# A selective scan with attention on one core: the order of exponential and u^T piece in ScalarE's queue

## The reference

```python
dt = softplus(proj[..., :512] + dt_bias)          # 512 channels
Bm, Cm = proj[..., 512:576], proj[..., 576:]       # 64 states
def step(hst, ins):
    dt_t, B_t, C_t, x_t = ins
    dA = exp(dt_t[:, :, None] * A)
    hst = hst * dA + (dt_t * x_t)[:, :, None] * B_t[:, None, :]
    y_t = einsum('bds,bs->bd', hst, C_t)
    return (hst, y_t)
```

## Time and profile before

| | us |
|---|---|
| median of 3 runs (3551.68 to 3552.13) | 3551.79 |
| the profiled execution, its time | 3553.52 |
| the profiled execution, its span | 3551.7 |
| of it busy: PE / VectorE / ScalarE / GpSimd | 3345.1 / 2983.3 / 2910.1 / 2304.6 |

### The profile page before, as it was taken

How to read it: one execution, slowest core, us unless ns; L and a number is a source line. 1 busy time by engine, 2 the same in 40 slices (tenths; PEclk the granted TensorE clock), 3 DMA queues, 4 the chain that set the end, 5 groups by cost and what they waited for, 6 DMA issues and landing times.

```text
span 3551.7 us, 59805 instructions
## 1 busy us (share of the span) xinstructions
PE 3345.1 (94%) x22946; PEld 2573.6 (72%) x22946; DVE 2983.3 (84%) x2916; ACT 2910.1 (82%) x4664; POOL 2304.6 (65%) x1066
## 2 busy tenths in 40 slices
PE   8998999899989999999999899999899989999999
PEld 5888888888888888988988888888787432222244
DVE  4988999899889989988999899899997488888241
ACT  5999999999998998999999999998896327777621
POOL 1878898898888879888988888798687000000000
PEclk9999999999999999999999999999899989999999
DMA  3222222222222222222222222222111052211000
GB/s 112 72 73 64 79 70 67 61 68 68 68 69 87 66 62 66 70 63 60 79 68 63 60 68 70 59 86 68 51 62 54 17 127 35 37 19 19 1 6 18
DMA packets 192638, 214.17 MB, mean 60 GB/s; under 512 B 75585, under 2 KB 144961, under 8 KB 192097
## 3 DMA queue, kind: packets, MB, share of 16 engines
q1 hardware_dynamic: 192354, 210.36, 20.6%
HBM read 192.19 MB, written 18.06 MB: 59 GB/s over the span
## 4 chain that ended last, share of the span: by engine, by line
PE 67%; ACT 19%; DVE 8%; issue 3%; POOL 2%; DMA 0%; SPq 0%; DVEq 0%; ACTq 0%; POOLq 0%
PE psum L1292 17%; PE psum L1513 16%; PE psum L1507 13%; PE psum L1504 10%; ACT arena L950 8%; ACT arena L933 6%; DVE arena L1198 4%; PE psum L1600 3%; PE psum L1589 3%; PE psum L1564 2%; DVE row_max L1245 2%; POOL arena L697 1%; PE psum L1533 1%; POOL arena L713 1%; ACT L950 1%
## 5 line engine op out<-in xcount | busy, mean ns | idle before, releaser
L1198 DVE TENSOR_TENSOR_SCAN arena<-arena,psum 128x512 f32<-128x512 f32 x2048 | 2379.0, 1229 | 192.1 <-ACT arena L950 105.8
L713 POOL TENSOR_TENSOR arena<-arena 128x1024 f32<-128x1024 f32 x1024 | 2237.5, 2192 | 458.1 <-DVE arena L1198 434.7
L950 ACT ACTIVATE arena<-arena,a_neg 128x512 f32<-128x512 f32 x2048 | 1436.5, 712 | 178.1 <-PE psum L1507 176.3
L1513 PE MATMUL psum<-ident,arena 128*128 128x128 f32 x8192 | 1244.4, 275 | 1.6 <-POOL arena L713 1.6
L933 ACT ACTIVATE arena<-arena,bT 128x512 f32<-128x512 f32 x1536 | 1091.9, 711 | 0.0
L1507 PE MATMUL psum<-ident,arena 128*128 128x128 f32 x6144 | 1021.7, 276 | 0.0
L1513 PEld LDWEIGHTS psum<-ident,arena 128*128 128x128 f32 x8192 | 974.8, 143 | 2.1 <-POOL arena L713 2.1
L1504 PE MATMUL psum<-arena 128*128 128x128 f32 x4096 | 844.5, 288 | 104.4 <-DVE arena L1198 89.8
L1504 PEld LDWEIGHTS psum<-arena 128*128 128x128 f32 x4096 | 656.2, 194 | 350.5 <-issue 185.6
L1507 PEld LDWEIGHTS psum<-ident,arena 128*128 128x128 f32 x6144 | 754.9, 144 | 0.0
L1292 PE MATMUL psum<-arena 128*128 128x512 f32 x1472 | 708.0, 604 | 29.4 <-ACT arena L813 18.3
(11 more groups left out here) (117 smaller groups left out, 1079.9 us busy)
## 6 DMA issues: line engine op xcount, KB each, us to landing
arena<-bc_dram SPq DMA_DIRECT2D x256, 512.0 KB, 3.7
arena<-diag_dram SPq DMA_DIRECT2D x224, 128.0 KB, 2.1
arena<-qk_dram SPq DMA_DIRECT2D x96, 128.0 KB
diag_dram<-arena SPq DMA_DIRECT2D x32, 256.0 KB, 4.5
qk_dram<-arena SPq DMA_DIRECT2D x12, 512.0 KB, 4.9
arena<-in_x SPq DMA_DIRECT2D x4, 512.0 KB, 10.9
arena<-in_up_w SPq DMA_DIRECT2D x1, 2048.0 KB, 11.7
out_xT<-arena SPq DMA_DIRECT2D x8, 256.0 KB, 2.2
```

What stands on the lines that cost most here:

```text
L713: pool.tensor_tensor(out[:, :, way], h_now[:, :, way], c_row, ALU.mult)\
L950: act.activation(decay[:, w % 2, f], dt_[:, u % 2, f], ACT.Exp, scale=a_neg[:, d, f, st:st + 1])\
L1198: dve.tensor_tensor_scan(hs[:, w % RING, f, rows][:, way], decay[:, w % 2, f, way], psum[:, 4 + n % U_BANKS, way], end_state(w - DS, f) if ...
L1513: return pe.matmul(psum[:, c, f * P:(f + 1) * P], hs[:, w % RING, f, at:at + P], ident[:, :], is_transpose=True, start=False, stop=w % DS ...
```

## The change

In each pair of ScalarE operations of the scan, `scan_input(w + 1, f)` is called ahead of the exponential of the same f instead of behind it:

```diff
                     if st == 0:
                         act.wait_ge(s["dt_ready"], NI + u)
                     for f in range(NI):
+                        if w + 1 < SCAN_TILES:
+                            scan_input(w + 1, f)
                         if w >= 2:
                             act.wait_ge(s["scan_done"], NI * (w - 2) + f + 1)
                         act.activation(decay[:, w % 2, f], dt_[:, u % 2, f], ACT.Exp, scale=a_neg[:, d, f, st:st + 1])\
                             .then_inc(s["decay_ready"], 1)
-                        if w + 1 < SCAN_TILES:
-                            scan_input(w + 1, f)
                     do(act_turns(u, st))
```

## The result

The changed kernel takes 3571.68 us (median of 5 runs, 3568.82 to 3576.25) against 3551.79 for the kernel before: a ratio of 1.0056, 95% interval 1.0042 to 1.0071. So it is slower by more than 0.2%, 5.3 us above the forecast and inside its range. The profiled execution has a span of 3569.9 us, 18.2 more than before.

The account below looks back on a forecast made before the run. PE or VectorE paces most stretches; ScalarE matters where late behind long operations, its wait for PE deciding. Terms 6.3 + 3.0 + 1.5 + 1.2 + 2.6 = +14.6 us on 3551.79 gave 3566.4 us; range 3556 to 3579.

Parts of the forecast that it names:

- the place of the gate: ScalarE's wait for PE's u turns moves ahead of each state's first exponential; pieces come no earlier, later exponentials 1.22 us later.
- Silu block: State 31, units 0 to 6: block 0.61 us later, PE has 0.14 to spare; 6 x 0.4 + 0.6 = 3.0 us.
- softplus block: State 46, units 0 to 6: start 0.61 us later, then exponentials 1.22 apart delay the fourth scan; 6.3 us in all.
- Tails: States 51 to 58 of units 2, 4, 6: exponentials 1.22 us later against slack of 0.62; 0.5 each, 1.5 us.
- The early drift: States 5 to 11: same drift as in states 51 to 58, no cost, since PE's products from state 11 cover it.
- Unit 0: State 18, where a square root interrupts ScalarE: costs as much as this unit's softplus block, 1.2 us.
- Unit 7: One root (state 25) and three table switches for the MLP's Silu: VectorE waits longer, 4 x 0.65 = 2.6 us.
- pieces come sooner and PE gains: Rival: PE's weight loads wait less for u^T pieces; 3530 us if half that wait lay on the path; chance 0.06.
- Hidden: Rival: Silu shift vanishes in PE's backlog, tails at the next unit's start; 4.3 us remains, 3556 us; chance 0.14.
- Exponentials as the bound of all even units' quiet states: Rival: a state's last exponential ends after its scan is due; 0.3 us in 100 states, 3596 us; chance 0.06.

Follow-up runs that it names:

- the gate-only kernel: Kernel before with only the wait for PE's turns moved ahead of each state's first exponential, all eight operations in their old order: 3578.48 us, ratio 1.0075.
- the order alone: Changed kernel with each state's first exponential kept ahead of the wait, pieces ahead of the other three exponentials: 3553.8 us, ratio 1.0003.
- the new order at the blocks alone: Kernel before with the changed kernel's order in states 31, 32, 46 and 47 of each unit: 3561.32 us, ratio 1.0025.
- the old order around the blocks: Changed kernel with the old order in states 31, 32, 46 and 47 of each unit: 3563.53 us, ratio 1.0031.
- the softplus held: Changed kernel with all four exponentials ahead of the wait and the softplus's second half issued behind the next state's exponentials: 3506.61 us, ratio 0.9861.
- state 30 in the old order: Changed kernel with the old order in states 30, 31, 32, 46 and 47 of each unit: 3562.09 us, ratio 1.0025.
- both blocks held: Changed kernel with all four exponentials ahead of the wait, softplus and Silu turns both issued behind the next state's exponentials: 3521.63 us, ratio 0.9903.

## Why the prediction was right, and where its terms were off

**What decides.** Right: the place of the gate. Moving the wait alone costs more than the change, leaving it and changing the order costs nothing, and moving it the other way gains in steps of the same size. The pieces' part shows too. With the gate in front, the new pair order is 7 us better than the old (3571.68 against 3578.48, two separate sets of runs): it makes the Silu block cheaper (0.1 to 0.3 us a unit instead of 0.6) and the softplus block dearer (6.2 in all instead of 4.4); the rest is mostly that two units more had the lower granted clock behind the Silus in the gate-only kernel. Whether the order had a part in that is not shown.

**Softplus block.** Right in size and in both parts: 6.2 us for 6.3. In the first part, 0.61 to 0.63 was measured at state 46 of units 1 to 6 for a forecast of 0.61. In the second, state 47, 0.34 in even units for 0.34; in odd units 0.05 for 0.14 (the forecast's own steps, 1322.95 less 1322.22, give 0.73 and not 0.75 in all, so 0.12), so VectorE's fourth scan had 0.1 us more in hand than I read.

**Silu block.** The largest miss: 5.1 us for 3.0. Three things in that step were off. "E(31,0) and E(31,1) stood back to back ..., as the gate opened" named the wrong wait: no idle time stands at them, and in the changed kernel ScalarE waits in state 30 and not in state 31. The shift was 0.61 all the same, which is luck in part: the gate of state 31 opens just when ScalarE arrives, so that either gate alone gives it. Then "of 0.61 PE has 0.14 to spare ... I take +0.4" was too dear: 0.1 was left in even units and 0.26 in odd ones where the granted clock was the same. In unit 3, scan(32,0)'s turn and the second one behind it stand 1.95 us apart after, against 2.20 before (1239.13 less 1236.93). These are its rows after:

```profile
1245.71 0.49 PE L1504 MATMUL psum<-arena 128*128 128x128 f32 x2 [1.41 <-DVE arena L1198]
...
1247.66 0.38 PE L1504 MATMUL psum<-arena 128*128 128x128 f32 x2
```

The pair took 0.86 from 1246.80 to the turn, not 0.97, and the piece was no longer late. The two runs that separate the causes agree: with the gate alone 0.61 to 0.63 stays in the units without the lower clock, so PE had nothing to spare for it, and with the order alone units 1 and 5 shrink by 0.3. At the same clock the block would have cost about 1.6 us in all, half of the forecast. The excess came from two units: in unit 1 the block cost 2.5 us and in unit 4 1.4, because PE was granted its lower level there, which it was not in the kernel before. Unit 1, the stretch behind the block, before and after:

```profile
580.00:587.00 7.00, 5.51 (x40) 4.40 (x39) 5.85 (x5) 6.99 (x13) 3.17 (x2) 1.00 0.20 75
```

```profile
581.00:588.00 7.00, 6.33 (x23) 4.66 (x23) 4.85 (x4) 6.99 (x12) 2.79 (x2) 0.53 0.17 64
```

No term of the forecast was for that. So the term came out 2 us short because a cost that I had not seen, 3.5 us, was larger than what I had charged too much.

**Tails.** 2.1 us for 1.5 in units 2, 4 and 6: each state of the drift costs 0.18, and the next unit's start hid little of it. The early drift came out at nothing as forecast, but not for the reason given: it is 0.16 to 0.2 in each of states 5, 7 and 9 of units 2, 4 and 6, and state 11 is shorter by 0.52 to 0.54. With the order alone there is no drift before it, and state 11 is shorter by 0.53 to 0.56 all the same; with the gate alone states 3 to 15 keep 0.6 in each of these units. So PE's products did not hide the drift: the gate costs 0.6 there and the order gains 0.55. That the term was right is luck.

**Unit 0.** 2.4 us for 1.2, the term being half of the true size. I had costed one interruption, at state 18; the trace shows growth in most states from 14 to 22, where ScalarE also waits at the copy of L936 that the change put ahead of E0 (15 waits, 22.1 us in the whole scan, against 14 and 19.2 before). The run with the order alone still has 1.6 us there, so in unit 0 the gate is not the only cause. A part goes with the granted clock: in these states PE had its lower level for 10.2 us before and for 13.6 after, with the gate alone and with the order alone. In the kernel with the new order at the blocks alone, where nothing in these states was changed, it had it for 6.8 us, and they shrink by 0.8. How much is the copy's own was not tried.

**Unit 7.** 1.6 us for 2.6. At three table switches I expected VectorE to wait longer, and it did, by 0.61 (0.66 with the next state, 2.0 us in all): after the last of them 1.81 us instead of the 1.20 of the earlier trace rows:

```profile
2621.15 9.53 DVE L1198 TENSOR_TENSOR_SCAN arena<-arena,psum 128x512 f32<-128x512 f32 x8 [1.81 <-ACT arena L952]
```

At the root the scans fall back by 0.61 in state 24 and gain 1.04 in states 27 to 31, so it counts -0.4. Here too the clock differs: the first of three stretches at the lower level was 6.8 us long before and 3.4 after. In the kernel with the old order around the blocks, which has the new order here and 6.8 us, 0.15 of the root's cost was left.

**The rivals.** That pieces come sooner and PE gains was half true: PE's weight loads do wait less, 22.8 us for 43.8. What that brings at single places (0.81 in state 0 of unit 1, 0.5 in state 11 of units 2, 4 and 6) is less than what the gate costs: with the order alone, where the gate costs nothing, the time is that of before. The rule of the Trainium skill, "Perfetto Trace Analysis", section "Optimization Strategy", to make the dependencies behind gaps start sooner, holds once one asks which operations need not wait: the exponentials do not need the gate, and the kernel that puts them all first gains 30 us, and 47 with the softplus held. "Hidden" fails at state 31, where five of the seven units kept 0.1 to 0.5 us of the Silu block's shift and two kept more, and in the tails. Exponentials as the bound of all even units' quiet states did not occur.

## What to carry to other kernels

In an in-order queue a wait also holds everything behind it: put what doesn't need the wait ahead of it, and look for the cost at the next long operation of that engine, not where the wait stands. Read where the engine last sat idle ahead of that block; from there on each operation that stands behind the wait costs its full spacing. Look at the next gates as well: one that opens just as the engine arrives shows no idle time and takes over as soon as the one ahead of it is cured. A wait that a change halves, here that of PE's weight loads, says nothing of the time until one knows that it ended the chain.

## What the runs showed of the hardware that was not expected

PE's granted clock behind the Silu block falls to its lower level in some units and not in others of the same kernel, and which ones changes with small shifts of the work. In units 1 to 6 a stretch of 6.8 us at 0.5 there was seen in no unit of the kernel before, in 1 and 4 of the changed one (the same two when it was profiled again), in 1, 2, 5 and 6 with the gate's wait alone, in 1, 3 and 5 with state 30 in the old order, and in none with all exponentials first or with the softplus held. The order alone had one in unit 3, the new order at the blocks alone in unit 1, two exponentials ahead in units 4 and 6, both blocks held in unit 6, and the old order around the blocks in none. Stretches of half that length, 3.4 us, came in further units, in units 2 and 6 before. Each of 6.8 us goes with 1.1 to 2.4 us more over states 31 to 35 than the units of the same kernel have without it (with both blocks held, 1.3 more than units with 3.4 us and 3.0 more than the one with none). What PE did just before does not decide it alone: in the changed kernel it stood 2.73 us for L813 in unit 1 (low after) and in unit 3 (not low):

```profile
580.28 1.13 PE L1292 MATMUL psum<-arena 128*128 128x512 f32 x2 [2.73 <-ACT arena L813]
```

```profile
1242.19 1.13 PE L1292 MATMUL psum<-arena 128*128 128x512 f32 x2 [2.73 <-ACT arena L813]
```

Between the first and the last scan the time lost to a lower clock (each stretch by the share not granted) was 61.8 us before, 66.5 after, 71.6 with the gate's wait alone and 48.1 in the fastest kernel. So by this estimate some 5 of the 16.9 us go with the clock. Whether the longer stands of PE cause it, or where they fall in time, is open and was not tried by itself.
